# DLRM tower on one core: interaction columns moved by DMA, ten tables looked up on the matmul engine

## What is computed

```
e = stack([tbl_f[ids[:, f]] for f in range(26)], axis=1)      # 2048 x 26 x 128
sd = einsum('bfd,bd->bf', e, dense)                            # 26 numbers per row
ss = einsum('bfd,bgd->bfg', e, e); pairs = ss[:, iu, ju]       # the 325 pairs f < g
z = concatenate([dense, sd, pairs], axis=1)
h = concatenate([z, dense], axis=1)                            # 607 columns
h = maximum(h @ W_top1 + b_top1, 0)                            # 512
h = maximum(h @ W_top2 + b_top2, 0)                            # 256
y = h @ W_top3                                                 # 2048 x 1
```

## Time and profile before

| | us |
|---|---|
| median of the 3 runs (403.44 to 405.14) | 403.52 |
| profiled execution | 404.94 |
| span of its instructions | 403.1 |
| PE busy | 337.3 (84%) |
| GpSimd busy | 277.5 (69%) |
| DVE busy | 234.1 (58%) |
| ACT busy | 204.8 (51%) |

### The profile page before, as it was taken

The page is one execution under the profiler, slowest core; times in us unless marked ns, Lnnn a source line. Parts: engine busy times, 40 slices in busy tenths (PEclk is TensorE's granted clock), DMA queues, the critical chain, the costliest instruction groups (busy, mean ns, idle before and its releaser), DMA issues.

```text
span 403.1 us, 14210 instructions
## 1 busy us (share of the span) xinstructions
PE 337.3 (84%) x6216; PEld 301.7 (75%) x6216; DVE 234.1 (58%) x702; ACT 204.8 (51%) x289; POOL 277.5 (69%) x295
## 2 busy tenths in 40 slices
PE   0556889898989889897989899896998989898585
PEld 0545679797878769795979779683987979796384
DVE  0969968682776438680867457670587538640321
ACT  2372545566466534666465553754346654565132
POOL 6777777777777777777777777777777777773000
PEclk9998989999999989999998999998899999899559
DMA  6998233222323214223323325122141323111000
GB/s 166 246 260 261 77 84 96 79 76 83 98 81 78 76 54 110 68 80 81 96 80 79 81 57 121 55 81 78 55 122 54 99 62 81 55 52 36 3 2 1
DMA packets 19118, 35.33 MB, mean 88 GB/s; under 512 B 7168, under 2 KB 8712, under 8 KB 19056
## 3 DMA queue, kind: packets, MB, share of 16 engines
q0 software_dynamic: 9216, 18.89, 17.8%
q1 hardware_dynamic: 9824, 15.52, 13.9%
q10 hardware_dynamic: 16, 0.01, 0.0%
HBM read 34.39 MB, written 0.01 MB: 85 GB/s over the span
## 4 chain that ended last, share of the span: by engine, by line
PE 55%; POOL 12%; ACT 11%; DMA 9%; issue 8%; DVE 3%; SPq 1%; POOLq 0%
PE et_ps L565 23%; POOL rows L290 12%; PE m_ps L525 10%; PE g_ps L486 8%; ACT et L371 8%; PE m_ps L536 6%; PE et_ps L555 5%; DMA et<-tbl_in 5%; DMA rows<-tbl_in,idx 3%; ACT zt_hi L346 2%; PE m_ps L545 2%; DMA idb<-ids_one_hot 1%; DVE one_hot L406 1%; DVE zt_lo L449 1%; DVE z L442 1%
## 5 line engine op out<-in xcount | busy, mean ns | idle before, releaser
L290 POOL DMA_INDIRECT rows<-tbl_in,idx x288 | 276.7, 961 | 89.3 <-issue 84.8
L406 DVE TENSOR_SCALAR one_hot<-idb,first_row 125x256 fp32r<-125x256 int32 x512 | 159.6, 384 | 81.5 <-PE et_ps L565 78.5
L371 ACT COPY et<-et_ps 128x384 f32<-128x384 f32 (+1 forms) x128 | 123.4, 1031 | 97.8 <-PE et_ps L565 76.7
L565 PE MATMUL et_ps<-one_hot,table_hi 125*128 125x256 f32 x512 | 132.7, 297 | 22.2 <-DVE one_hot L406 18.8
L565 PE MATMUL et_ps<-one_hot,table_lo 125*128 125x256 f32 x512 | 127.1, 286 | 0.0
L565 PEld LDWEIGHTS et_ps<-one_hot,table_hi 125*128 125x128 f32 x512 | 100.1, 195 | 29.2 <-issue 20.4
L565 PEld LDWEIGHTS et_ps<-one_hot,table_lo 125*128 125x128 f32 x512 | 100.0, 195 | 0.0
L555 PE MATMUL et_ps<-ident,rows 128*128 128x128 f32 x288 | 51.1, 291 | 16.6 <-DMA rows<-tbl_in,idx 11.9
L486 PE MATMUL g_ps<-et 128*27 128x26 f32 x4096 | 54.0, 193 | 11.4 <-issue 9.2
L486 PEld LDWEIGHTS g_ps<-et 128*27 128x27 f32 x4096 | 45.3, 106 | 23.0 <-issue 15.9
L555 PEld LDWEIGHTS et_ps<-ident,rows 128*128 128x128 f32 x288 | 32.6, 145 | 22.3 <-issue 13.1
(11 more groups left out here) (46 smaller groups left out, 284.5 us busy)
## 6 DMA issues: line engine op xcount, KB each, us to landing
idb<-ids_one_hot SPq DMA_DIRECT2D x32, 256.0 KB
rows<-tbl_in,idx POOLq DMA_INDIRECT x288
et<-tbl_in SPq DMA_DIRECT2D x7, 448.0 KB
xt<-dense_t SPq DMA_DIRECT2D x8, 128.0 KB, 3.9
z<-w_z SPq DMA_DIRECT2D x2, 256.0 KB, 5.9
et<-w SPq DMA_DIRECT2D x1, 512.0 KB, 6.9
gram<-tbl_in SPq DMA_DIRECT2D x1, 448.0 KB
et<-tbl_in SPq DMA_DIRECT2D x7, 52.0 KB
```

Source lines behind the costliest of these rows:

```text
L290: nc.gpsimd.indirect_dma_start(out=rows[:, r, n, :], out_offset=None, in_=tables[GATHERED[k]], in_offset=bass.IndirectOffsetOnAxis(idx[par ...
L371: nc.scalar.copy(dst, src).then_inc(et_copied, 1)
L406: last = nc.vector.tensor_scalar(one_hot[n % 2][0:KP, k, :], idb[0:KP, n // 2 % ID_RING, n % 2, :], first_row[0:KP, 0:1], float(k), ALU.su ...
L565: last = nc.tensor.matmul(ps[:, n % 2 * CH:n % 2 * CH + CH], part[0:KP, n, k, :], one_hot[n % 2][0:KP, k, :], start=k == 0 and part is tab ...
```

## The change

The list of steps is new, and with it the staging of nearly everything around it:

- Two more tables of 1000 rows (16, 17) go by one-hot products: 10 tables, 16 gathered. The gathered ones fill slots of four (`SIZES`), 8 steps `T` a chunk in place of 12; the ring has 6 slots of 4.
- `A`, `Z` and DVE's copies to `z` are gone. The batch is laid out so that a quarter q of the partitions of `gram` holds a quarter of the chunk's rows, and after the last gram copy nine blocks of columns go straight from `gram` to `zt_raw` by DMA, four transfers a block (steps `D`, 36 a chunk): two quarters from SP and two from ACT, in the last chunk four in all from GpSimd. `Z` is now ACT's split only, and DVE's behind it.
- The first layer is cut by input block (`X0` dense, `K0` to `K2` the three blocks of z) and accumulates in both banks; its bias is a row of the weights against a row of ones.
- The first five one-hot tables of a chunk are looked up a phase ahead (`AHEAD`); `et` is a ring of three tiles of 128 rows, not two of 256; four banks `et_ps`, not two; one-hot slices go through a ring of 12 with a semaphore step each, not two buffers of 8.
- Five tables are staged at once at the start, not two.

```diff
-SCHEDULE = [(step[0], int(step[1:])) for step in (
-    "O0 B2 G4 O1 B3 G5 T0 G6 O2 B4 G7 O3 B5 A0 T1 A1 O4 O5 A2 T2 A3 T3 Z0 Z1 T4 T5 Z2 B6 B7 L0 T6 L1 T7 "
-    "O6 O7 T8 L2 G0 T9 G1 G2 T10 G3 T11 L3").split()]
+PHASE = (
+    "O5 G4 G5 G6 G7 T0 O6 D0 D1 D2 D3 X0 O7 T1 D4 D5 D6 O8 Z0 D7 D8 K0 T2 O9 Z1 T3 K1 Z2 G0 G1 O0 G2 G3 "
+    "K2 T4 O1 T5 M0 O2 Y0 O3 T6 O4 T7").split()
...
+SIZES = (4, 4, 4, 4)
...
+OH_RING = 12
+ROW_RING = 6
...
+        def move_block(eng, c, n, quarters, landed=z_in):
+
+            i0, width, part, at = BLOCKS[n]
+            for q in quarters:
+                src = gram[c % GRAMS][32 * q + i0 + 1:32 * q + FW, i0 * GROUPS:(i0 + width) * GROUPS]
+                dst = zt_raw[at:at + width * (F - i0), part, q * GROUPS:(q + 1) * GROUPS]
+                eng.dma_start(dst, src.rearrange("j (i g) -> j i g", i=width)).then_inc(landed[part], 16)
...
+                if kind == "D":
+                    if n == 0:
+                        await_gram(act, c)
+                    move_block(act, c, n, quarters_of("A", c, n))
+                if kind == "Z":
+                    late = landed_late(n) if c == NCH - 1 else 0
+                    wait(act, z_in_late[n], late)
+                    act.wait_ge(z_in[n], (c + 1) * LANDED[n] - late)
...
+                    wait(act, h1_sums, 2 * c)
+                    nc.scalar.copy(zt_parts[0][:, n, :], zt_raw[:, n, :]).then_inc(zt_hi_done, 1)
...
+                if kind == "K":
+                    pe.wait_ge(zt_split, c * KZ + n + 1)
+                    first_layer(c, n + 1)
```

## The result

| | before | after |
|---|---|---|
| time, median of 4 runs | 403.48 us (402.34 to 405.14) | 457.72 us (455.93 to 461.19) |
| span of the profiled execution | 403.1 | 456.4 |
| mean granted clock of TensorE | 0.95 | 0.91 |
| a chunk, in the steady part | 45.5 us | 51.2 us |

The ratio is 1.135 (95% interval 1.127 to 1.143): 13.5% slower. The forecast was 394.4 us, faster, in a range that ended at 413. In two of the later runs (e10_spread2, e15_spread_busy9) one execution, the one that was profiled, was in a slower state with a lower granted clock; their medians leave it out, and from their profiles no clock is read.

What follows compares the result with a forecast made beforehand. GpSimd's gathers were taken as the bound, 45.6 us a chunk. Head 75.5, six chunks at 43.3 (259.8), last phase 33.7 and end 25 made a span of 394.0, median 394.4 us; range 372 to 413.

Steps and rivals of the forecast that it cites:

- The bound moves from GpSimd to PE's waits: Steady chunk: GpSimd's gathers fall to 40.5 us, PE's own work stands at 40.0, so PE's waits set the chunk.
- ACT and K0: First layer's first z block: PE waits 1.1 us a chunk for ACT's split behind its queued moves; upper case 3.2.
- The clock behind the wait: PE after K0's wait: half clock for 3 us costs 1.5, in two chunks of three; counted only in the slower case.
- rival 2: ACT becomes the bound: moves run behind its copies, K0 waits 3.2 us, chunk 46.4, median 416 us; chance 17%.
- K1: First layer's second z block: PE waits 1.2 us a chunk for ACT's split behind a copy, bounds 0.9 and 1.7.
- Gram run: G4 to G7 in a row: PE waits 1.0 us a chunk with nothing named (issue), bounds 0 and 2.7.
- Chunk: Steady chunk: PE's work 40.0 plus waits 1.1, 1.2 and 1.0 make 43.3 us, against 45.6 before.
- Last phase: Last phase before the end: six tables fewer, an open copy and a second gram run make 33.7 us.
- Head: Start to chunk 0's G7: DVE builds the tables, PE follows, late ids add up to 3; 75.5 us (74 to 79).
- Transfers and their flight: Moves from gram to zt_raw: 0.031 us a piece, landing 3.9 us, there before ACT comes; flight costs nothing in chunks.
- End: From the last G7 to the result: copy, 18 issues on SP, landing, split, layers; 25 us.
- rival 4: Costs cancel: chunk 44.3 to 44.9 us, the slower head eats the gain, 401.5 to 405.5 us; chance 8%.

Runs made afterwards that it cites:

- e10_spread2: Against the kernel with moves spread over the phase: T3 ahead of O9, K0 before the gram run, K1 after O3, G0 to G3 in a row; 445.94 us.
- e15_spread_busy9: Against the kernel with moves spread over the phase: 9 idle matmuls added ahead of G0; 428.14 us, ratio 1.060.

## Why the prediction was wrong

By the prediction's own steps. The span came out 62.4 us longer than its sum (456.4 for 394.0): 2.9 before the first move of chunk 0, 47 in six chunks, 9.6 in the last phase and 2.8 after the first move of the last chunk.

- **The bound moves from GpSimd to PE's waits**: right. PE's own work was put at 40.0; at full clock it is 39.8 to 40.4 (the run without moves). GpSimd stalls for PE's transposes from 40 us on.
- **"ACT and K0", 1.1 us, is the term that failed.** It measured 5.15 us on average. The mechanism was the forecast's own, moves queued ahead of the split on ACT; the price was wrong. The forecast took 0.22 us an issue from one ACT row, or 0.40 from one SyncE row, and "nearer the ACT row, since it is the same engine". Both rows are transfers between SBUF and HBM whose patterns had nothing in common with the new ones. That 8 of the 14 moves "cost nothing" under O6 and X0 fell with the price: they keep ACT's queue for 6.5 us. With 0.81 us the layout by hand gives the wait at once: moves begin at 1.0, fourteen take 11.3, hi and lo of the split 0.40 and 0.43: 13.1, against PE at 8.2: 4.9 us. So 4.05 us a chunk of the miss is this one price, and the upper bound of 3.2 was none, since 0.40 was not an upper bound for a kind of transfer that the trace didn't have.
- **The clock behind the wait** stood only in rival 2, with 1.0 us a chunk. It costs some 2 us in every chunk (1.9 by the run with 22 idle matmuls). It also comes behind some shorter waits: two of six chunks without any moves have it, behind waits of 1.6 and 1.7 us for issue, while K1's wait of 1.5 us never calls it in the changed kernel.
- **K1**, 1.2: measured 1.5, in each chunk. **Gram run**, 1.0: measured 0.8 to 1.3 in these chunks. Both terms held.
- **Chunk**: 43.3 was forecast and 51.2 measured, 7.9 more: 4.05 (K0), about 2.0 (clock), 0.3 (K1), and some 1.5 that no single wait explains. About half of that are PE's gaps under 0.6 us (0.7 a chunk), and the rest lies in its busy time, 42.7 us a chunk against the 40.0 forecast, beyond the clock's 2.0. It isn't DVE's one_hot: the 20.4 us on line 522 all lie before 92 us. Six chunks make 47.
- **Last phase**, 33.7: measured 43.3. The same K0 wait (4.58) and clock, and three waits ahead of parts of the gram, 1.91, 1.89 and 2.02 us, where 1.5 in all had been counted; together they make the difference.
- **Head**: G7 of chunk 0 was to end at 75.5, and the first move to follow at 76.5; it came at 79.36. DVE's late ids (4.7 us before 51 us) and PE's wait of 2.4 us for one_hot at 62.8 had been cost at "up to 3" together.
- **SP**, no bound: right, though its 0.44 us an issue stands in no row; it measured 0.79, so 18 moves are 14.3 us a chunk.
- **Transfers and their flight**, nothing: right. GpSimd's four moves land 1.8 us after their start in three cases and 3.7 in one. SyncE's landings aren't in the profile, but in the run with all moves on it the split starts 1.6 to 2.8 us, in the median 1.9, after the last move of its block began. Both are below the 3.9 assumed, and what PE waits for is the issuing ahead of it. The Trainium skill, "DMA: Bandwidth & Descriptors" (Anatomy of one DMA), gives a fixed cost of about 2.0 us for a transfer that GpSimd issues; GpSimd's 1.8 agrees. Its section "Issuing engines are not separate DMA queues" says that issuing from several engines saves only the sequencer's time, "usually small relative to the DMA itself". Here an issue of 0.8 us stands beside some 1.9 from its start to the landing, and without the 36 issues a chunk the loss is gone (404.03); the runs decide against "small".
- **End**: 25 from the last G7, which is 24 from the first move of the last chunk; that measured 26.8, 2.8 over.

Rival 2 was the right story, with half the real price of an issue: 416 us where 457.7 came. It had 17%. The chance that deserved more room was not another mechanism, but the unknown price of a new kind of transfer, with 18 of them on an engine that also paces PE. And rival 4 was right in a way that the text didn't see: even with moves for nothing the head, the waits and the falls of the clock eat the whole gain (404.03 us, run once). By this run the forecast of 394.4 would have missed by 10 us with a perfect price.

What stays open: what makes a transfer of this kind cost 0.6 to 0.9 us of its queue. Size doesn't order the blocks, but one thing about their shape does. In the run with all moves on SyncE the medians by block are 0.60, 0.69, 0.66 and 0.63 us where a move reads 16, 8, 4 and 2 partitions, and 0.79, 0.79, 0.81, 0.80 and 0.84 where it reads 12, 20, 22, 24 and 26. The powers of two are the cheap ones in the changed kernel too (0.66 to 0.73 against 0.79 to 0.88) and in the run with one column a move (0.62 to 0.70 against 0.74 to 0.83). Why is not shown, and it is 0.1 to 0.2 us of the price; the other 0.6 is in every block. A transfer of another direction was not tried in its place. One transfer for all four quarters of a block would cut the issues to nine a chunk; it was not tried.

## What to carry to other kernels

Price a transfer by its issue on the queue, times the number of transfers, and ask what else stands in that engine's program behind it; a row of another kind of transfer doesn't bound that price from above (0.22 and 0.40 us in the rows, 0.8 here). When the bound moves from an engine that runs steadily to PE with waits, the half clock is a second price: some 2 us behind each wait of 5 us here, and now and then behind waits of 1.6 to 1.9. And before costing a replacement, look at what the best case leaves: here free transfers gave the old time.

## What the runs showed of the hardware

- A small SBUF to SBUF transfer occupied its queue for 0.77 to 0.80 us (median) on SyncE and on ACT, 0.62 on GpSimd (four in the tail), alike with or without the other queue issuing. Moves that read 2, 4, 8 or 16 partitions took 0.60 to 0.73, those that read 12 to 26 took 0.79 to 0.88 (medians by block). Loads of ids from HBM on SyncE took 0.33 (median), those of dense features 0.49.
- On ACT the issue did not stop the running instruction (copies of 1.25 us ran beside it), but all that stood behind it in the program: a copy whose bank was full at 187.4 us started at 188.79.
- Behind each of PE's seven waits of 4.6 to 6.0 us the clock was granted at 0.50 for some 5 us, behind some of its waits of 1.6 to 1.9 us for some 3, behind K1's seven waits of 1.5 us never. Filling the wait of 5 us with 22 matmuls that nobody needs kept the clock at 1.00 there and made the whole kernel 13 us faster.
- A matmul of 96 fp32 columns took 0.22 us of PE and stands in the profile as two of 0.11; a transpose of 128 columns in the same kernel took 0.09 and stands as one.
